# Vision-transformer layer on one core: VectorE's half of the query/key projection becomes a step of its own, one slot behind the products and ScalarE's conversion

## The chip, the core and the metric

One core of a Trainium2 chip runs the whole program. The metric is the device time of one execution in microseconds, as the median of three runs. TensorE (PE in the profile) multiplies, ScalarE (ACT), VectorE (DVE) and GpSimd (POOL) work elementwise, and SyncE (SP) and ScalarE issue the transfers. TensorE writes its results to eight PSUM banks. Each engine works through its own list of instructions in order. Semaphores tie the lists together.

## What is computed

64 images of 12 channels and 224x224 pixels are pooled in patches of 16x16, which gives 196 tokens for each image. A first attention follows, then an expert layer whose second stage contains an attention of 12 heads with 16 dimensions each. What matters here is that second attention:

```python
h = jnp.einsum('becd,fd->becf', xg, w1) + b1          # routed tokens times w1
h = jnp.einsum('becn,becf->bnf', dispatch, h)
x_mlp, x_qkv = (h[..., :MLP_HID], h[..., MLP_HID:])
q, k, v = ...                                         # from x_qkv, 12 heads of 16
attn = jax.nn.softmax(jnp.einsum('bhqd,bhkd->bhqk', q, k) * scale, axis=-1)
x_attn = jnp.einsum('bhqk,bhkd->bhqd', attn, v)
x_mlp = jax.nn.gelu(x_mlp, approximate=False)
```

q and k are kept as two float16 numbers each: the rounded value (high part), and what was rounded away (low part), so that float16 products of three stacked blocks come near float32.

## The kernel before

**Groups, images, slots.** The 64 images go through in 8 groups of 8. The text counts both from 0, so group 2 is the third. The body of a group has 96 slots, 12 for each image, one for each head. In slot h of image i, TensorE makes the products `peak` of head h for image i+1 (line L937). VectorE takes their row maxima (`peaks`, L1459), with which the softmax will be shifted. TensorE also makes the products `score` of head h for image i (L956), and ScalarE takes the exponential (L1155). 8 further slots, the opening of the next group, hold the MLP products `hidden` (L909) with ScalarE's Gelu (L1133), and the peaks of that group's first image.

**The projection.** `project` of image i+2 stands in slot 1 of image i. TensorE computes q and k into two banks (L919). ScalarE rounds each to float16 (L1142, the high part). VectorE subtracts the high part from the bank and writes the low part (L1448), and only then gives the bank back. SyncE waits for both parts, writes them to the scratch tensor `qk_scratch` in HBM (L683), waits for that transfer, and reads six blocks back into the stacks `qs` and `ks` (L689), which the peaks of image i+2 need from slot 0 of image i+1 on. In the opening, `project` of image 1 stands first. For image 0 it stands in the last slots of the group before.

**Banks.** Two of the eight banks serve the peaks in turn (h even, h odd), two the scores. The other four, called the ring, serve everything else. `plan_ring` walks through the list of steps and gives each the ring bank that has been closed longest. TensorE waits before a ring step until the bank's previous user has been read out.

**Fill.** Between peaks and scores stand the other steps: `norm_turn` (L980 on TensorE, then L1470 and L1472 on VectorE, two halves in slots 2 and 3), `norm_back`, `fc2` (L1002), `mix` (L971), and for the next group the pooling of its images: `pool` on VectorE (L1267, seven steps for each tile `xt`, after the last of which the next tile is fetched), and the routing steps (`take`, `norm1`, `first_max` with L1308, `gate_scale` with L1359 and others). Two tables `VECTOR` and `TENSOR` hold a cost for each step in each engine's time. The function `evenly` places the pool steps where the sum of TensorE's costs in a slot exceeds that of VectorE's.

**Peaks and their banks.** The matmul of head h waits until the maxima of head h-2 have been taken, since both use the same bank. VectorE's list in slots 1 to 3 therefore decides when TensorE can start heads 3, 4 and 5.

Of the kernel before, what the change touches and what calls it, by code (L numbers as in the profile page):

```python
# [201 lines left out]
def turning(dg, at):  # L202


    ops = [(at, ("turn_u", dg, 0)), (at + 0.5, ("turn_u", dg, 1)), (at + 1, ("project", dg, 0))]
    return ops + [(at + 1 + 0.5 * i, ("turn_u", dg, i)) for i in range(2, GRP)]


# [25 lines left out]
def opening(dg, tail):  # L234


    plan = []
    last = GRP - 1
    for i in range(GRP):
        ops = []  # L240
        plan.append(ops)
        if tail:
            if i == 0:
                ops.append(("mix", dg - 1, last, H // QUAD - 1))
            if i == 1:
                ops += [("norm_turn", dg - 1, last, half) for half in range(2)]
            if i == 2:
                ops.append(("norm_back", dg - 1, last))
            if 2 <= i < 2 + FC2 // 2:
                ops += [("fc2", dg - 1, last, k) for k in range(2 * (i - 2), 2 * (i - 2) + 2)]  # L250
        if i == 5:
            ops.append(("gate8", dg))
        if i == 0:
            ops.append(("project", dg, 1))
        ops.append(("hidden", dg, i))
        if i == 1:
            ops.append(("values", dg, 0))
        if 1 <= i < 7:
            ops += [("peak", dg, 0, h) for h in range(2 * (i - 1), 2 * (i - 1) + 2)]
        if i == 4:  # L260
            ops.append(("shift", dg, 0, 0))
    ops.append(("shift", dg, 0, 1))
    return plan
# [3 lines left out]
TAKE = 27  # L267
VECTOR = {"peak": 0.52, "choose": 0.95, "first_max": 0.52, "take": 0.9, "norm1_scale": 0.9, "norm1": 0.8, "shift1": 1,
          "stream": 0.9, "stream_norm": 1.2, "gate_scale": 0.2, "gate_logits": 1.8, "gates": 2, "gate_rows": 0.4,
          "chosen": 0.3, "spread": 2.9, "project": 1.3, "norm_turn": 0.65, "fc2": 0.75, "gate8": 1.2, "tok": 0.25}  # L270
TENSOR = {"peak": 0.35, "score": 0.35, "mix": 0.65, "fc2": 0.89, "hidden": 2, "project": 1.33, "values": 0.66,
          "residual": 0.66, "norm_turn": 0.4, "norm_back": 0.34, "shift": 0.2, "turn_u": 0.18, "planes": 1, "tok": 0.15,
          "first_max": 0.66, "first_exp": 0.66, "first_mix": 0.7, "stream": 0.25, "stream_turn": 0.2,
# [3 lines left out]
def body(pool_next, with_next):  # L277
# [3 lines left out]
    for i in range(GRP):  # L281
        fill = [[] for h in range(H)]
# [12 lines left out]
            fill[10] = [("values", 0, i + 1)] + fill[10]  # L295
        if i + 2 < GRP:
            fill[1] = [("project", 0, i + 2)] + fill[1]
        for h in range(H):
            ops = []
            plan.append(ops)  # L300
            if i + 1 < GRP:
                ops.append(("peak", 0, i + 1, h))
            ops.append(("score", 0, i, h))
            ops += fill[h]
            if h in (MIX_LAG, QUAD + MIX_LAG):
                ops.append(("mix", 0, i, h // QUAD - 1))
            if i and h == MIX_LAG - 4:
                ops.append(("mix", 0, i - 1, H // QUAD - 1))
# [7 lines left out]
    front, at = routing(1, TAKE)  # L316
    for slot, op in in_slots(front):
        plan[slot].append(op)
    at = rounds(plan, 1, int(at))
# [4 lines left out]
    at = evenly(plan, pieces * (GRP // PAIR - AHEAD), 0, TAKE - 4)  # L324
# [3 lines left out]
    if pool_next:  # L328
        at = evenly(plan, pieces * AHEAD, TAKE + 1, len(plan) - 3, quiet)
# [8 lines left out]
def ring_of(op):  # L338
    name, key = op[0], op[1:]
    if name == "hidden":  # L340
        ks = [("hid", key + (b,)) for b in range(NF // 2)]
        return ks, ks
    if name == "project":
        ks = [("q", key), ("k", key)]
        return ks, ks
    if name == "mix":
        ks = [("O", key)]
        return ks, ks
    if name == "fc2":
        g, i, k = key  # L350
# [45 lines left out]
def bass_vit_tower(nc, x, cw, Wq, bq, Wk, bk, Wv, bv, w_router, gamma, beta, w1, b1, w2, b2, consts, out):  # L396
# [8 lines left out]
    with ctx:  # L405
# [775 lines left out]
        def _(dve):  # L1181
# [13 lines left out]
            k = 2  # L1195
# [243 lines left out]
                chain(at, dve.tensor_tensor(gate8[:, :, 0:1], cg[:, :, 0:1], gate8[:, :, 1:2], ALU.add))  # L1439
                linked("gate8", 5)  # L1440

            def project(at, G_, dg, i):

                for m in range(2):
                    slot, k_ = at.uses(("qk"[m], (dg, i)))
# [32 lines left out]
            def fc2(at, G_, dg, i, k_):  # L1478
                if k_ == FC2 - 1:
# [3 lines left out]
                    for h in range(2):  # L1483
# [9 lines left out]
                      "first_max": first_max, "shift1": shift1, "stream": stream, "stream_norm": stream_norm,  # L1493
                      "gate_scale": gate_scale, "gate_logits": gate_logits, "gates": gates,
                      "gate_rows": gate_rows, "choose": choose, "chosen": chosen, "spread": spread,
                      "gate8": gates8, "project": project, "peak": peak, "norm_turn": norm_turn, "fc2": fc2})


        @block.gpsimd
# [79 lines left out]
```

How the kernel before makes its waits and increments, by code:

```python
        @block.sync  # L648
# [13 lines left out]
            sp.dma_start(wr_in[:, :], w_router).then_inc(w_in, 16)  # L662
            for m, b in enumerate((gamma, beta)):
                for c in range(2):
                    sp.dma_start(gb[:, m, c:c + 1], b[DC * c:DC * c + DC].rearrange("(p a) -> p a", a=1)) \
                        .then_inc(w_in, 16)
            sp.dma_start(w1_in[:, 0:10, :], w1[0:1280, :].rearrange("(f p) d -> p f d", p=128)).then_inc(w_in, 16)
            sp.dma_start(w1_in[0:F1 - 1280, 10, :], w1[1280:F1, :]).then_inc(w_in, 16)
            sp.dma_start(w2_in[:, :, :], w2.rearrange("(o p) f -> p o f", p=DC)).then_inc(w_in, 16)
            sp.dma_start(b1_in, b1.rearrange("(a f) -> a f", a=1)).then_inc(w_in, 16)
            sp.dma_start(b2_in[:, 0:2, :], b2.rearrange("(a o f) -> a o f", a=1, o=2)).then_inc(w_in, 16)
            sp.wait_ge(su_act, 2)
            sp.dma_start(G[C:2 * C, :], Vp).then_inc(su_dma, 16)
            sp.wait_ge(turn_free, NT - 1)
            sp.wait_ge(su_dve, 4)
# [2 lines left out]
            def project(at, G_, dg, i):  # L678
                n_ = G_ * GRP + i
                sp.wait_ge(hi_ready, 2 * n_ + 2)
                sp.wait_ge(lo_ready, 2 * n_ + 2)
                sp.dma_start(qk_dram[i % 2].rearrange("m s c d (h t) -> (d h) (m s c) t", t=T),
                             qk16[:, :, :, :, :].rearrange("p m s c t -> p (m s c) t")).then_inc(qk_out, 16)
                sp.wait_ge(qk_out, 16 * n_ + 16 + ONE)
                s = i % NSTACK
```

## Time and profile before

| | before |
|---|---|
| median of 3 runs | 1855.82 us (1848.53 to 1863.67) |
| the profiled execution's own time | 1857.67 us |
| its span, first to last instruction | 1855.8 us |
| mean granted TensorE clock | 0.897 |
| TensorE busy | 1525.9 us (82%) |
| VectorE busy | 1215.5 us (65%) |
| ScalarE busy | 846.7 us (46%) |
| GpSimd busy | 249.2 us (13%) |

The profile comes from one execution. Busy means that an instruction of the program was in work. A row of the timeline joins neighbouring instructions of one line; the number in square brackets is the idle time of the engine just before it, and behind the arrow stands what ended it. Shares are means over stages that differ, so that a term of the sum is always read in its own stage.

### The profile page before, as it was taken

Reading aid. Unit: us, or ns where it says so; the run is one execution under the profiler, and the core shown is the slowest. Engines: PE = TensorE matmul, PEld = TensorE weight load, DVE = VectorE, ACT = ScalarE, POOL = GpSimd, SP = SyncE. Lnnn points to the kernel's source line nnn. Section 1 sums busy time; section 2 is a strip of 40 time slices with the busy share of each in tenths; the row PEclk is TensorE's granted clock in tenths of the full one; section 3 lists DMA queues with packets and bytes.
Section 4 is the critical chain, followed back from the end, with each engine's and each line's share of the span. In section 5 each row is a group of like instructions: output and inputs, shape, how many; then the busy total and the mean of one; then the engine's idle time right before and its main releaser. Section 6 shows DMA issues by size and latency. Waiting matters only on the chain.

```text
span 1855.8 us, 34563 instructions
## 1 busy us (share of the span) xinstructions
PE 1525.9 (82%) x12440; PEld 1252.8 (68%) x12440; DVE 1215.5 (65%) x2822; ACT 846.7 (46%) x1935; POOL 249.2 (13%) x318
## 2 busy tenths in 40 slices
PE   4214188998889898998899898989989899989998
PEld 3103176777777677777777677867777687868786
DVE  3366847785877657784877667784777757573552
ACT  1001054544545455544645455544545456545653
POOL 2002101220012001210012001120022101110000
PEclk8556578999999899998999899997899899999999
DMA  3797635542656155542646155642656152101220
GB/s 77 198 231 186 182 82 143 142 131 64 173 128 175 49 150 145 145 128 71 174 128 166 49 154 141 155 121 57 162 137 173 49 150 50 41 25 43 54 57 15
DMA packets 99598, 218.03 MB, mean 117 GB/s; under 512 B 61371, under 2 KB 75877, under 8 KB 88678
## 3 DMA queue, kind: packets, MB, share of 16 engines
q10 hardware_dynamic: 12288, 154.15, 31.5%
q1 hardware_dynamic: 87142, 61.68, 14.4%
q8 instruction: 102, 1.67, 0.4%
q14 instruction: 66, 0.54, 0.1%
HBM read 186.57 MB, written 28.90 MB: 116 GB/s over the span
## 4 chain that ended last, share of the span: by engine, by line
PE 37%; DVE 26%; issue 21%; DMA 7%; POOL 4%; ACT 3%; SPq 0%; DVEq 0%; ACTq 0%; POOLq 0%
DVE psums L1267 9%; DVE peaks L1459 6%; PE bank L1002 6%; PE bank L909 5%; PE bank L971 4%; DMA xt<-in_x_dram 4%; PE bank L919 3%; POOL var L1522 3%; PE bank L937 3%; DMA qs<-shiftT 3%; PE bank L956 2%; PE bank L835 2%; PE bank L819 2%; DVE rows L1403 2%; DVE top L1398 1%
## 5 line engine op out<-in xcount | busy, mean ns | idle before, releaser
L1459 DVE TENSOR_REDUCE peaks<-bank 98x2 f32<-98x392 f32 x768 | 424.6, 562 | 185.8 <-PE bank L937 164.9
L1155 ACT ACTIVATE Pb<-bank 98x392 f32<-98x392 f32 x768 | 374.7, 497 | 290.7 <-PE bank L956 250.1
L1267 DVE TENSOR_REDUCE psums<-xt 112x2 f32<-112x512 f32 x672 | 430.1, 678 | 74.7 <-DMA xt<-in_x_dram 52.6
L937 PE MATMUL bank<-ks,qs 96*98 96x196 f16 x1536 | 265.4, 259 | 59.5 <-DMA ks<-qk_scratch 31.6
L1002 PE MATMUL bank<-w2T,hid 128*98 128x192 f32 x1536 | 301.9, 335 | 0.0
L956 PE MATMUL bank<-qs,ks 97*98 97x196 f16 x1536 | 267.0, 258 | 9.9 <-DMA qs<-shiftT 9.2
L937 PEld LDWEIGHTS bank<-ks,qs 96*98 96x98 f16 x1536 | 165.8, 127 | 143.0 <-DVE peaks L1459 50.4
L1002 PEld LDWEIGHTS bank<-w2T,hid 128*98 128x98 f32 x1536 | 240.3, 170 | 1.7
L971 PE MATMUL bank<-Pb,vals 98*32 98x196 f32 x3072 | 181.5, 357 | 11.6 <-ACT Pb L1155 11.6
L956 PEld LDWEIGHTS bank<-qs,ks 97*98 97x98 f16 x1536 | 167.5, 130 | 20.1 <-DMA qs<-shiftT 10.7
L1448 DVE TENSOR_TENSOR qk<-bank,qk 96x392 f16<-96x392 f32 x128 | 71.8, 561 | 137.9 <-ACT qk L1142 129.5
L1550 POOL TENSOR_TENSOR fin<-fin,both 98x384 f32<-98x384 f32 x64 | 63.8, 997 | 651.9 <-DVE fin L1484 651.9
L909 PE MATMUL bank<-UT,M 104*128 104x196 f32 x768 | 143.6, 338 | 0.0
L909 PEld LDWEIGHTS bank<-UT,M 104*128 104x128 f32 x768 | 132.6, 197 | 2.6 <-issue 2.2
L971 PEld LDWEIGHTS bank<-Pb,vals 98*32 98x32 f32 x3072 | 84.5, 114 | 72.5 <-issue 48.1
L1133 ACT ACTIVATE hid<-bank 128x392 f32<-128x392 f32 x192 | 93.9, 497 | 83.0 <-PE bank L909 82.5
L1513 POOL TENSOR_TENSOR spread_p<-psums,cst 112x196 f32<-112x196 f32 x96 | 49.9, 520 | 595.7 <-DVE psums L1267 595.3
L786 PE MATMUL bank<-spread_p,cst 112*24 112x196 f32 x192 | 49.2, 406 | 97.9 <-POOL spread_p L1513 97.9
L1067 ACT COPY oT<-bank 128x196 f32<-128x196 f32 x192 | 61.9, 322 | 132.0 <-PE bank L971 127.1
L1002 PE MATMUL bank<-w2T,onT 96*98 96x192 f32 (+1 forms) x512 | 106.7, 331 | 8.5 <-ACT onT L1067 8.5
L919 PE MATMUL bank<-UT,M 104*96 104x196 f32 x512 | 111.8, 368 | 0.1
L786 PEld LDWEIGHTS bank<-spread_p,cst 112*24 112x24 f32 x192 | 20.4, 120 | 118.2 <-issue 112.4
(181 smaller groups left out, 1826.2 us busy)
## 6 DMA issues: line engine op xcount, KB each, us to landing
xt<-in_x_dram ACTq DMA_DIRECT2D x96, 1568.0 KB, 8.9
qk_scratch<-qk SPq DMA_DIRECT2D x64, 294.0 KB, 4.1
qs<-qk_scratch SPq DMA_DIRECT2D x192, 73.5 KB, 2.9
ks<-qk_scratch SPq DMA_DIRECT2D x192, 73.5 KB, 3.0
out_dram<-fin SPq DMA_DIRECT2D x64, 147.0 KB
qs<-shiftT SPq DMA_DIRECT2D x128, 2.3 KB
hid<-in_L_ffn_w_dram SPq DMA_DIRECT2D x1, 1440.0 KB
hid<-in_L_ffn_w_dram SPq DMA_DIRECT2D x1, 960.0 KB
```

The lines of the kernel that those rows point to most:

```text
L786: mm = pe.matmul(ps[0:PAIR * C, 0:T], const("plane", PP)[:, PAIR * C * t:PAIR * C * t + PAIR * C], spread_p[:, t, :, :].rearrange("p a b - ...
L909: mm = pe.matmul(ps[:, T * j:T * j + T], M[:, 128 * f:128 * f + 128], UT[:, i, :], start=True, stop=True)
L919: mm = pe.matmul(ps[0:DC, T * c:T * c + T], M[:, f:f + DC], UT[:, i, :], start=True, stop=True)
L937: mm = pe.matmul(peak_ps[s][0:HT, T * q:T * q + T], qs[0:KS, i % NSTACK, h, HT * q:HT * q + HT], ks[0:KS, i % NSTACK, h, :], start=True, s ...
L956: mm = pe.matmul(score_ps[s][0:HT, T * k:T * k + T], ks[:, i % NSTACK, h, HT * k:HT * k + HT], qs[:, i % NSTACK, h, :], start=True, stop=True)
L971: mm = pe.matmul(ps[32 * j:32 * j + 32, 0:T], vals[:, i % 2, q, h, :], Pb[:, (H * i + h) % NP, q, :], start=(q == 0), stop=(q == 1))
L1002: mm = pe.matmul(misc_ps[slot][0:HT, D * h:D * h + D], lhs, w2T[0:w, f, :], start=(f == 0), stop=(f == NF + 1))
L1133: act.activation(hid[:, i, 2 * b:2 * b + 2, :].rearrange("p a b -> p (a b)"), ps[:, 0:2 * T], ACT.Gelu).then_inc(free, 1)
L1155: act.activation(Pb[:, (H * i + h) % NP, :, :].rearrange("p a b -> p (a b)"), score_ps[s][0:HT, 0:2 * T], ACT.Exp, scale=float(DH) ** -0.5 ...
L1267: last = dve.tensor_reduce(psums[:, m % 2, t, 2 * p:2 * p + 2], v[:, 2 * p:2 * p + 2, :, :], AX.XY, ALU.add)
L1448: dve.tensor_tensor(qk16[:, m, 1, :, :].rearrange("p c t -> p (c t)"), misc_ps[slot][0:DC, 0:2 * T], qk16[:, m, 0, :, :].rearrange("p c t ...
L1459: dve.tensor_reduce(peaks[:, h // 6, :, h % 6], peak_ps[s][0:HT, 0:2 * T].rearrange("p (q k) -> p q k", q=2), AX.X, ALU.max, negate=True). ...
```

## The change

`project` stays where it is on TensorE, ScalarE and SyncE. VectorE's function is renamed `low` and becomes a step with a place of its own. For image i+2 that is slot 2 of image i, ahead of `norm_turn`. In the opening it stands behind both halves of `norm_turn`, and in the last slots of a group one slot later than before. The body of VectorE's function is unchanged. The two banks of q and k are opened by `project` and closed by `low`, so that two of the four ring banks are held by them over all steps that lie between. The cost 1.3 moves from the entry `project` of `VECTOR` to an entry `low`, so that `evenly` sees more room in slot 1 and less in slot 2.

```diff
-    ops = [(at, ("turn_u", dg, 0)), (at + 0.5, ("turn_u", dg, 1)), (at + 1, ("project", dg, 0))]
+    ops = [(at, ("turn_u", dg, 0)), (at + 0.5, ("turn_u", dg, 1)), (at + 1, ("project", dg, 0)), (at + 1.8, ("low", dg, 0))]
...
         if i == 0:
             ops.append(("project", dg, 1))
+        if i == 1:
+            ops.append(("low", dg, 1))
         ops.append(("hidden", dg, i))
...
-          "chosen": 0.3, "spread": 2.9, "project": 1.3, "norm_turn": 0.65, "fc2": 0.75, "gate8": 1.2, "tok": 0.25}
+          "chosen": 0.3, "spread": 2.9, "low": 1.3, "norm_turn": 0.65, "fc2": 0.75, "gate8": 1.2, "tok": 0.25}
...
         if i + 2 < GRP:
             fill[1] = [("project", 0, i + 2)] + fill[1]
+            fill[2] = [("low", 0, i + 2)] + fill[2]
...
     if name == "project":
-        ks = [("q", key), ("k", key)]
-        return ks, ks
+        return [("q", key), ("k", key)], []
+    if name == "low":
+        return [], [("q", key), ("k", key)]
...
-            def project(at, G_, dg, i):
+            def low(at, G_, dg, i):
...
-                      "gate8": gates8, "project": project, "peak": peak, "norm_turn": norm_turn, "fc2": fc2})
+                      "gate8": gates8, "low": low, "peak": peak, "norm_turn": norm_turn, "fc2": fc2})
```

**VectorE, slots 0 to 3 of image 0 in a group's body, where image 2 is projected.** `qk16` is the low part, `psums` a pool step, `peaks` the maxima of one head. Before:

```order
L1459 TENSOR_REDUCE peaks<-bank2 98x2
L1459 TENSOR_REDUCE peaks<-bank3 98x2
L1448 TENSOR_TENSOR qk16<-bank4,qk16 96x392
L1448 TENSOR_TENSOR qk16<-bank5,qk16 96x392
L1459 TENSOR_REDUCE peaks<-bank2 98x2
L1267 TENSOR_REDUCE psums<-xt 112x2
L1459 TENSOR_REDUCE peaks<-bank3 98x2
```

After:

```order
L1463 TENSOR_REDUCE peaks<-bank2 98x2
L1463 TENSOR_REDUCE peaks<-bank3 98x2
L1271 TENSOR_REDUCE psums<-xt 112x2 x2
L1463 TENSOR_REDUCE peaks<-bank2 98x2
L1452 TENSOR_TENSOR qk16<-bank4,qk16 96x392
L1452 TENSOR_TENSOR qk16<-bank5,qk16 96x392
L1463 TENSOR_REDUCE peaks<-bank3 98x2
```

The low part now stands behind the maxima of head 2 and ahead of those of head 3. Two pool steps stand where it was; before, one followed head 2.

**TensorE, the first two slots of an opening.** L919 (L923) is the projection of q and k, L909 (L913) one pair of `hidden` products, L980 (L984) one half of `norm_turn`, L926 (L930) the values. Banks 4 to 7 are the ring. Before:

```order
L919 MATMUL bank6<-UT,M 96x196 x2
L919 MATMUL bank4<-UT,M 96x196 x2
L909 MATMUL bank5<-UT,M 128x196 x2
L909 MATMUL bank7<-UT,M 128x196 x2
L909 MATMUL bank6<-UT,M 128x196 x2
L980 MATMUL bank4<-cst,oT 98x128 x3
L980 MATMUL bank5<-cst,oT 98x128 x3
L909 MATMUL bank7<-UT,M 128x196 x2
L909 MATMUL bank6<-UT,M 128x196 x2
L909 MATMUL bank4<-UT,M 128x196 x2
L926 MATMUL bank5<-M,UT 98x192 x2
```

After:

```order
L923 MATMUL bank4<-UT,M 96x196 x2
L923 MATMUL bank7<-UT,M 96x196 x2
L913 MATMUL bank5<-UT,M 128x196 x2
L913 MATMUL bank6<-UT,M 128x196 x2
L913 MATMUL bank5<-UT,M 128x196 x2
L984 MATMUL bank6<-cst,oT 98x128 x3
L984 MATMUL bank5<-cst,oT 98x128 x3
L913 MATMUL bank6<-UT,M 128x196 x2
L913 MATMUL bank5<-UT,M 128x196 x2
L913 MATMUL bank4<-UT,M 128x196 x2
L930 MATMUL bank7<-M,UT 98x192 x2
```

TensorE's steps are the same in the same order, on other banks. Between the projection and the third step of the second image's `hidden`, everything now shares banks 5 and 6.

**VectorE, slots 1 to 3 of image 5, where image 7 is projected.** L1359 (L1363) is `gate_scale`, for whose result GpSimd waits. Before:

```order
L1459 TENSOR_REDUCE peaks<-bank3 98x2
L1448 TENSOR_TENSOR qk16<-bank5,qk16 96x392
L1448 TENSOR_TENSOR qk16<-bank4,qk16 96x392
L1267 TENSOR_REDUCE psums<-xt 112x2
L1459 TENSOR_REDUCE peaks<-bank2 98x2
L1470 RECIPROCAL rden<-bank6 98x12
L1472 TENSOR_TENSOR on_tok<-bank6,rden 98x192
L1359 TENSOR_SCALAR var<-var 98x16
L1459 TENSOR_REDUCE peaks<-bank3 98x2
```

After:

```order
L1463 TENSOR_REDUCE peaks<-bank3 98x2
L1271 TENSOR_REDUCE psums<-xt 112x2 x2
L1463 TENSOR_REDUCE peaks<-bank2 98x2
L1452 TENSOR_TENSOR qk16<-bank7,qk16 96x392
L1452 TENSOR_TENSOR qk16<-bank4,qk16 96x392
L1474 RECIPROCAL rden<-bank6 98x12
L1476 TENSOR_TENSOR on_tok<-bank6,rden 98x192
L1363 TENSOR_SCALAR var<-var 98x16
L1463 TENSOR_REDUCE peaks<-bank3 98x2
```

One more pool step stands ahead of `gate_scale`, and the low part has moved behind head 2.

Elsewhere the pool steps have moved by a slot or two. The one that the prediction speaks of: of the two pool steps in slots 10 and 11 of image 2, one stood on either side of the maxima of image 3's last head, and both stand ahead of it now. An opening holds 15 pool steps in place of 16.

## Rows read from the trace of the kernel before

**Rows 1.** Waits: engine and line, released by, us in total, times, longest.

```profile
PE bank L937 <- DMA ks<-qk_scratch: 31.6, 8, 5.5
...
PE bank L937 <- DVE peaks L1459: 25.0, 35, 2.0
```

**Rows 2.** Groups by line and form: busy us, mean ns, idle before.

```profile
L1267 DVE TENSOR_REDUCE psums<-xt 112x2 f32<-112x512 f32 x672 | 430.1, 678 | 74.7 <-DMA xt<-in_x_dram 52.6 <-DVE peaks L1459 7.6 <-DVE qk L1448 4.8
...
L1448 DVE TENSOR_TENSOR qk<-bank,qk 96x392 f16<-96x392 f32 x128 | 71.8, 561 | 137.9 <-ACT qk L1142 129.5
```

**Rows 3.** Timeline (start, us, engine, line), group 2, projection of image 2.

```profile
688.36 1.27 DVE L1448 TENSOR_TENSOR qk<-bank,qk 96x392 f16<-96x392 f32 x2 [1.33 <-ACT qk L1142]
...
689.77 0.57 DVE L1459 TENSOR_REDUCE peaks<-bank 98x2 f32<-98x392 f32 x1
690.26 0.68 DVE L1267 TENSOR_REDUCE psums<-xt 112x2 f32<-112x512 f32 x1
...
690.39 0.37 PE L937 MATMUL bank<-ks,qs 96*98 96x196 f16 x2 [1.80 <-DVE peaks L1459]
...
691.46 0.37 PE L937 MATMUL bank<-ks,qs 96*98 96x196 f16 x2 [0.53 <-DVE peaks L1459]
```

**Rows 4.** Windows of the same place: busy us by engine, then granted clock.

```profile
688.40:691.80 3.40, 1.08 (x11) 0.68 (x9) 3.11 (x6) 1.59 (x4) 0.00 (x0) 1.00 0.55 132
691.80:695.20 3.40, 3.40 (x26) 1.98 (x24) 1.92 (x4) 1.57 (x4) 0.00 (x0) 0.50 0.25 60
```

**Rows 5.** Timeline of the opening behind group 1.

```profile
656.37 0.56 DVE L1448 TENSOR_TENSOR qk<-bank,qk 96x392 f16<-96x392 f32 x1 [5.26 <-ACT qk L1142]
...
656.86 2.56 PE L909 MATMUL bank<-UT,M 104*128 104x196 f32 x12
...
658.90 1.27 ACT L1133 ACTIVATE hid<-bank 128x392 f32<-128x392 f32 x3
659.25 0.82 PE L980 MATMUL bank<-cst,oT 128*98 128x128 f32 x6
...
659.93 2.23 PE L909 MATMUL bank<-UT,M 104*128 104x196 f32 x12
```

**Rows 6.** Timeline of group 2, projection of image 4.

```profile
730.33 0.56 DVE L1448 TENSOR_TENSOR qk<-bank,qk 96x392 f16<-96x392 f32 x1 [0.39 <-ACT qk L1142]
...
731.39 0.57 DVE L1459 TENSOR_REDUCE peaks<-bank 98x2 f32<-98x392 f32 x1
...
732.66 0.57 DVE L1459 TENSOR_REDUCE peaks<-bank 98x2 f32<-98x392 f32 x1
...
733.67 0.33 PE L937 MATMUL bank<-ks,qs 96*98 96x196 f16 x2
```

**Rows 7.** Timeline of group 2, slot 0 of image 3.

```profile
748.39 0.33 PE L946 MATMUL bank<-cst,peaks 98*6 98x98 f32 x2 [0.53 <-DVEq L1464]
```

**Rows 8.** Timeline of group 2, slots 2 and 6 of image 5.

```profile
804.75 0.18 DVE L1359 TENSOR_SCALAR var<-var 98x16 f32<-98x16 f32 x1
...
805.01 2.90 POOL L1522 TENSOR_TENSOR var<-var,cst 98x16 f32<-98x16 f32 x1 [7.96 <-DVE var L1359]
...
809.83 0.89 PE L1002 MATMUL bank<-w2T,onT 96*98 96x192 f32 x4 [1.25 <-ACT onT L1067]
```

**Rows 9.** Timeline of group 7, the last, projection of image 4.

```profile
1748.46 0.57 DVE L1459 TENSOR_REDUCE peaks<-bank 98x2 f32<-98x392 f32 x1
...
1749.48 0.33 PE L937 MATMUL bank<-ks,qs 96*98 96x196 f16 x2
```

**Rows 10.** Timeline of group 2: image 3's parts out, the six reads, their wait.

```profile
704.42 0.31 SPq L683 DMA_DIRECT2D qk_scratch<-qk  x1
...
711.86 0.31 SPq L689 DMA_DIRECT2D qs<-qk_scratch  x1
...
723.33 0.56 PE L937 MATMUL bank<-ks,qs 96*98 96x196 f16 x2 [5.14 <-DMA ks<-qk_scratch]
```

**Rows 11.** Page, DMA issues: KB each, median us from issue to landing.

```profile
qk_scratch<-qk SPq DMA_DIRECT2D x64, 294.0 KB, 4.1
```

## Prediction, made before the changed kernel had run

> **What bounds the kernel now.** I read the groups by line first. VectorE stands idle 129.5 us in front of the low part L1448, waiting for ScalarE's conversion [rows 2]. That looks like a prize of 7% of the span, but only TensorE's idle time counts, because TensorE is busy 82% of the span. So I read its waits next: what it loses to late maxima is 25.0 us of matmul idle time in all, in 35 places, and 31.6 us in 8 places go to the transfer of the stacks [rows 1]. The question is which of VectorE's 129.5 us are TensorE's too.
>
> The timeline answers it image by image. For image 2 they are: VectorE waits 1.33 us, subtracts until 689.63, takes head 2's maxima at 689.77, and TensorE stands 1.80 us before head 4 and 0.53 us before head 5 [rows 3]. The windows show the consequence: TensorE works 1.08 us of the 3.40 us from 688.4, at the full clock, and the next 3.40 us are granted 0.50, which is 1.2 GHz [rows 4]. Eight groups at 2.33 us make 18.6 us, so most of the 25.0 us is here. The 5.26 us at the opening [rows 5] delay nobody: TensorE runs from 656.86 to 662.16 without an idle microsecond between its rows. For the other images VectorE waits 0 to 1.6 us at the low part, as at image 4 [rows 6], and no wait of TensorE for the maxima of head 4 by more than about 0.2 us follows: there the wait is filled time that costs nothing.
>
> **The change, part by part.** The same 128 subtractions of 0.56 us run [rows 2]. No transfer is added. What changes is who stands behind whom.
>
> *Image 2 (gain).* Without the low part, VectorE is free at 687.03, that is 688.36 less the 1.33 idle. Two pool steps of 0.68 [rows 2] now fill the wait, to 688.4; head 2's maxima take 0.57, to 688.95, and TensorE starts head 4 at 689.0 rather than 690.39. Then comes the low part, 1.27 us to 690.2, then head 3's maxima to 690.8, and TensorE starts head 5 at 690.85 rather than 691.46 [rows 3]. The wait moves from head 4 to head 5, and 0.6 us a group is left of the 2.33. The low part ends 0.6 us later, so its stack does too. In four groups that stack landed with less than 1 us to spare and in two it was already waited for, which takes back a part. I take -4 us for 8 groups, between 0 and -5. The clock is a further question, a rival below: TensorE would still stand still for some 1.6 of 2.3 us, which I take as too little better to keep the clock up.
>
> *The opening (loss).* q and k hold two ring banks until both halves of `norm_turn` are through VectorE. The first image's third `hidden` product now shares bank 5 with its first, and must wait for the first Gelu, which ends at 658.90 + 0.50 = 659.4. Before, it had q's bank, free at 656.93, and its four matmuls began near 658.6 in the run of twelve that ends at 659.42 [rows 5]: +0.9 us. Those four then end near 660.35, and their Gelu takes 0.5, to 660.9. The second half of `norm_turn` uses the same bank, and TensorE would be ready for it at 660.5: +0.4. The second image's `hidden` needs both banks of `norm_turn` read by VectorE, another 0.2 to 0.3. The sum is 1.65 us, with bounds 0.9 (only the Gelu wait stays) and 1.9. Behind it TensorE is busy nearly without a break, so nothing gives it back. Seven openings at 1.65 and the first at 1.0 (no `norm_turn`) make +12.6 us. A rule of the Trainium skill speaks against the change here as well: its page "Perfetto Trace Analysis", section "Matmul Optimizations", asks that all eight PSUM banks be used so that work can overlap. By it, the loss is every step that finds fewer free banks; by the rows, only the opening has consecutive ring steps so dense that it is felt, and the sum is as above.
>
> *Image 4 (loss).* Before, the low part ended at 730.89, in time that VectorE had free since the projection came late; then head 2's maxima at 731.39, head 3's at 732.66, done 733.23, ahead of TensorE's head 5 at 733.67 [rows 6]. Now the low part, 1.27 us, and the 0.14 us behind it (689.63 to 689.77 in [rows 3]) stand between head 2 and head 3, whose maxima end at 733.23 + 1.41 = 734.64. TensorE's head 5 waits 1.0 us. The tiny steps of routing behind it go 1.4 us later and could add 0.4 (they feed a GpSimd step that TensorE waits for). Bounds 0 and 1.4, since a later wait for another cause could swallow it; I take 1.0 in seven groups, +7 us.
>
> *Slot 0 of image 3 (loss).* TensorE already waits 0.53 us there for the maxima of the last head of the image before [rows 7]. One more pool step, 0.68, now stands ahead of them; about 0.6 shows. Pool steps of this stretch exist in six groups: +3.5 us, bounds 0 and 4.
>
> *Image 7 (loss).* `gate_scale` at 804.75 starts GpSimd's 2.90 us, on which `gate_logits`, then ScalarE's exponential, then the copy onT hang, for which TensorE waits 1.25 us at 809.83 [rows 8]. One pool step more stands ahead, and the low part has only changed places: +0.7 us in six groups, +4 us, bounds 0 and 4.5.
>
> *The last group (loss).* No pool steps fill anything. Image 4's head 3 ends its maxima at 1749.03, head 5 starts at 1749.48 [rows 9]. The low part's 1.41 us go in between, less 0.4 that I allow for head 2 coming earlier, since it no longer waits for the low part: head 3 ends at 1750.05. That is +0.57 us for images 3 to 7, +3 us, bounds 0 and 4.
>
> *Images 3, 5 and 6 (nothing).* VectorE waited 0.1 to 0.8 us there; the pool step gained and the low part lost cancel within 0.3 us. SyncE issues image 3's write at 704.42, and the reads at 711.86, 7.4 us later [rows 10]; the write shares the engines with a tile fetched on ScalarE's queue, and lands with it. Issued 1 to 1.6 us later it still has 5.8 us, more than the median write's 4.1 [rows 11], so the stall of 5.14 us stays as it is. The cover is that fetch; without it, the full 1 to 1.6 us would show in six groups, +6 to 10 us.
>
> Sum: -4 + 12.6 + 7 + 3.5 + 4 + 3 = +26 us. The profiled execution took 1857.67 (span 1855.8 and 1.9 around it), 1.85 above the median, so 1855.8 + 26 = 1882 us. Low bounds: -5 + 7 + 0 = 1858. High bounds: 0 + 14.5 + 10 + 4 + 4.5 + 4 = +37, 1893.
>
> **The rivals.** *Swallowed.* Each loss lands just ahead of a wait for something else and vanishes, and only the opening's Gelu wait, 8 x 0.9 = 7 us, and the gain of 4 stay: 1859. For it: TensorE idles a sixth of the span in all. Against it: between the places named its rows follow each other closely. *The clock pays (faster).* At image 2 TensorE does four `peak` matmuls sooner, the 3.40 us at clock 0.50 do not follow, and up to half of them, 1.7 us, comes back, in up to seven groups: -12 us, with the gain of 5 -17. It decides the sign once the losses stay under 17 us, as when the opening costs 0.9 and image 4 nothing: 1855.8 - 17 + 7 = 1846; with no loss at the banks at all, 1839. Against it: at that place the stack of image 2 has less than 1 us to spare in four groups, so that TensorE would run into that transfer. The Trainium skill ("TensorE: Matmul & The Clock Gate", section "What's actually happening") says that the clock falls back after idleness and not by chance; the trace agrees, 1.08 us of work in 3.40 ahead of the fall. *The stack grows late.* The write of image 3 is pushed behind the fetch: 1882 + 8 = 1890, and more where image 2's stack joins it, to 1900. *Nothing moves on VectorE.* ScalarE's part is so late that the low part still waits where it stands now: only the bank costs are left, 1868. Against it: at image 2 ScalarE releases VectorE at 688.36 [rows 3], before VectorE would come to it at 688.95.
>
> **How the numbers follow.** Chances: the forecast 0.54 (1866 to 1893), swallowed 0.2 (1850 to 1866, with the variant in which nothing moves on VectorE), the clock pays 0.16 (1828 to 1850), the stack grows late 0.1 (1893 to 1905). Predicted is the first, 1882. The range 1846 to 1897 leaves out most of the third and half of the fourth, 2 in 10. A measurement of this kernel tells about 1%, 18.6 us, from no change: faster is below 1837.3, slower above 1874.4. Slower: 0.42 of the forecast and 0.1, 0.52. Faster: 0.1, from the third. Same: 0.38.
>
> **What would show it.** In the changed profile the low part's idle time should fall from 137.9 us to under 70. TensorE's wait for the maxima should leave head 4 of image 1's row and appear at head 5 there (about 1.2 us) and at image 4 (1.0). In each opening a wait of the L909 matmuls for ScalarE's Gelu of 0.7 to 0.9 us should be new. The wait of L946 at slot 0 of image 3 should be about 1.1, that for onT about 1.9. The prediction is wrong if the openings keep their length, or if the 0.50 stretch behind image 2 is gone in most groups.

## The result, and the profile after

| | before | after |
|---|---|---|
| median | 1858.82 us (4 runs, 1848.53 to 1863.67) | 1882.88 us (4 runs, 1870.31 to 1887.49) |
| ratio | | 1.0137, 95% interval 1.0096 to 1.0179 |
| the profiled execution, its span | 1857.67, 1855.8 us | 1884.72, 1882.9 us |
| mean granted clock in it | 0.897 | 0.901 |
| VectorE's low part: busy, idle before it | 71.8, 137.9 us | 71.4, 61.2 us |

The changed kernel is slower by 24 us. Some executions of either kernel are in a slower state, and every comparison below leaves them out. VectorE waits 77 us less in front of the low part (61.2, forecast under 70), and TensorE, busy 82% of the span in both, gets none of it.

Groups by line and form of the changed kernel (busy us, mean ns, idle before), answering [rows 2]:

```profile
L1452 DVE TENSOR_TENSOR qk<-bank,qk 96x392 f16<-96x392 f32 x128 | 71.4, 558 | 61.2 <-ACT qk L1146 51.2
```

TensorE's waits in the changed kernel (us in total, times, longest), answering [rows 1]:

```profile
PE bank L790 <- POOL spread_p L1517: 95.6, 12, 26.7
PE bank L941 <- DMA ks<-qk_scratch: 37.7, 13, 5.6
...
PE bank L941 <- DVE peaks L1463: 22.4, 50, 1.0
...
PE bank L913 <- ACT hid L1137: 6.6, 6, 1.9
...
PE bank L1006 <- DVEq L1457: 3.6, 12, 0.4
...
PE bank L984 <- ACT hid L1137: 1.8, 7, 0.3
```

The maxima are waited for oftener and shorter (longest 1.0 for 2.0 us). The transfer of the stacks is waited for in 13 places instead of 8, and three rows of bank and Gelu waits are new. For spread_p the sum is lower only because the part ahead of the loop differs from run to run; its count went from 6 to 12.

Timeline of group 2, projection of image 2 (start, us, engine, line), answering [rows 3]:

```profile
696.68 1.26 DVE L1452 TENSOR_TENSOR qk<-bank,qk 96x392 f16<-96x392 f32 x2
...
696.82 0.37 PE L941 MATMUL bank<-ks,qs 96*98 96x196 f16 x2 [0.21 <-DVE peaks L1463]
...
698.71 0.37 PE L941 MATMUL bank<-ks,qs 96*98 96x196 f16 x2 [1.04 <-DVE peaks L1463]
...
707.38 0.37 PE L941 MATMUL bank<-ks,qs 96*98 96x196 f16 x2 [1.67 <-DMA ks<-qk_scratch]
```

Windows of the same place (busy us by engine, granted clock, DMA share, GB/s), answering [rows 4]:

```profile
696.60:700.00 3.40, 2.04 (x17) 1.36 (x20) 2.95 (x7) 2.09 (x6) 0.00 (x0) 1.00 0.33 74
700.00:703.40 3.40, 3.40 (x50) 2.15 (x42) 3.40 (x7) 2.97 (x8) 0.00 (x0) 1.00 0.21 47
```

The wait of 1.80 us at head 4 is gone (0.21), that at head 5 has grown from 0.53 to 1.04, and image 2's stack is now waited for, 1.67 us in this group. In the first window TensorE works 2.04 us, for 1.08 before, and its clock does not fall to 1.2 GHz behind it here.

The opening behind group 1, answering [rows 5]:

```profile
663.26 1.49 PE L913 MATMUL bank<-UT,M 104*128 104x196 f32 x8
...
665.25 0.89 ACT L1137 ACTIVATE hid<-bank 128x392 f32<-128x392 f32 x2
665.80 0.93 PE L913 MATMUL bank<-UT,M 104*128 104x196 f32 x4 [1.05 <-ACT hid L1137]
...
666.57 0.49 PE L984 MATMUL bank<-cst,oT 128*98 128x128 f32 x3
667.32 0.53 PE L984 MATMUL bank<-cst,oT 128*98 128x128 f32 x3 [0.26 <-ACT hid L1137]
667.93 2.34 PE L913 MATMUL bank<-UT,M 104*128 104x196 f32 x12
...
668.66 1.27 DVE L1452 TENSOR_TENSOR qk<-bank,qk 96x392 f16<-96x392 f32 x2
...
670.78 0.50 PE L941 MATMUL bank<-ks,qs 96*98 96x196 f16 x4
```

From the first `hidden` product to the first peaks of the new group's first image (L941) the opening takes 7.52 us, for 5.78 before, where these peaks start at 662.64. Up to `norm_turn` it is 3.31 us (663.26 to 666.57) for 2.39, and from there to the second image's `hidden` 1.36 for 0.68 (659.25 to 659.93 in [rows 5]):

```profile
662.64 0.50 PE L937 MATMUL bank<-ks,qs 96*98 96x196 f16 x4
```

**Where the time went, image by image.** The table lists, summed over the groups, by how much each stretch from one image's first `peak` matmul to the next image's is longer than in the first profile of before. Each number comes from the starts of these matmuls in the timelines and is good to about 0.5 us. Stretch 7 holds the first part of the next opening too, up to the new group's first peaks; what follows, up to image 1's, is equal in all kernels. (The expectations call a stretch an image's period: that of image 6 is stretch 6.)

```
stretch                   1      2      3      4      5      6      7
before, second profile  -0.8   -2.0   -0.3    0.0   +1.4   +0.3   -4.1
changed                 -8.7   -2.4   +7.7   +5.4   +1.5  +14.8  +14.0
changed, second         -5.4   -6.1  +10.1   +5.5   +1.7  +13.1   +7.9
e1_open_back            +5.1   -0.5   +6.8   +5.4   +1.3  +13.1   +1.8
e2_open_only            +2.0   -2.3    0.0    0.0   -0.4   +0.4  +13.6
e3_cost_back            -2.0   +1.5  +10.6   +0.7   +2.1   +2.8   +4.3
e4_cost_only           +20.9   -1.4   -2.3   +4.9   -2.0  +13.9   -8.3
f1_planes_later         -7.7   -5.1   +9.2   +5.4   +1.4   +5.2   +9.4
f2_image2_only          -2.1   -2.5   +3.2   +0.1   +0.6   -1.2   +1.9
f3_banks_only           +2.1   +0.6   +1.2   +0.1    0.0   +0.5   +8.9
f4_image4_back          +3.5   +0.2   -1.9   +2.0  +10.7   +5.9   +5.4
g1_image2_pool          -4.4   +0.4   +0.1    0.0   +0.3   +0.2    0.0
```

Stretches 3 to 6 repeat within about 2.5 us between two profiles of one kernel. Stretches 1, 2 and 7 hold most of the falls of the clock and repeat only within about 6 us. The part ahead of image 0's first peaks took 240 to 253 us, and is not in the table, nor is the first opening, which lies in it.

### The profile page after: what moved, and what is told of

It is laid out like the page before. It is cut to its first block, busy times and chain, and to the rows that moved or that the text cites. A ratio compares the mean times of both kernels' runs of the same rounds, so it can differ in the third digit from the quotient of the medians.

```text
span 1882.9 us, 34563 instructions
## 1 busy us (share of the span) xinstructions
PE 1537.9 (82%) x12440; PEld 1250.0 (66%) x12440; DVE 1216.1 (65%) x2822; ACT 849.5 (45%) x1935; POOL 248.7 (13%) x318
## 3 DMA queue, kind: packets, MB, share of 16 engines
q10 hardware_dynamic: 12288, 154.15, 30.4%
q8 instruction: 102, 1.67, 0.4%
## 4 chain that ended last, share of the span: by engine, by line
PE 42%; DVE 23%; DMA 14%; issue 13%; POOL 3%; ACT 2%; SPq 2%; DVEq 0%; POOLq 0%; ACTq 0%
PE bank L1006 7%; DVE psums L1271 6%; DVE peaks L1463 6%; PE bank L913 5%; PE bank L975 5%; PE bank L923 4%; DMA ks<-qk_scratch 4%; DMA xt<-in_x_dram 3%; PE bank L941 3%; DMA qk_scratch<-qk 3%; PE bank L960 3%; DMA qs<-shiftT 3%; PE bank L839 2%; POOL var L1526 2%; PE bank L790 2%
## 5 line engine op out<-in xcount | busy, mean ns | idle before, releaser
L941 PE MATMUL bank<-ks,qs 96*98 96x196 f16 x1536 | 265.2, 259 | 62.1 <-DMA ks<-qk_scratch 37.7
L1006 PE MATMUL bank<-w2T,hid 128*98 128x192 f32 x1536 | 305.4, 338 | 3.7 <-DVEq L1457 3.6
L941 PEld LDWEIGHTS bank<-ks,qs 96*98 96x98 f16 x1536 | 164.3, 126 | 148.7 <-issue 49.4
L1006 PEld LDWEIGHTS bank<-w2T,hid 128*98 128x98 f32 x1536 | 242.0, 171 | 8.7 <-DVEq L1457 6.7
L913 PE MATMUL bank<-UT,M 104*128 104x196 f32 x768 | 147.5, 342 | 7.6 <-ACT hid L1137 6.6
L913 PEld LDWEIGHTS bank<-UT,M 104*128 104x128 f32 x768 | 132.1, 197 | 15.2 <-ACT hid L1137 9.0
L790 PE MATMUL bank<-spread_p,cst 112*24 112x196 f32 x192 | 49.1, 405 | 95.6 <-POOL spread_p L1517 95.6
L1006 PE MATMUL bank<-w2T,onT 96*98 96x192 f32 (+1 forms) x512 | 106.4, 330 | 8.8 <-ACT onT L1071 8.8
L923 PE MATMUL bank<-UT,M 104*96 104x196 f32 x512 | 112.8, 370 | 0.1
L1452 DVE TENSOR_TENSOR qk<-bank,qk 96x392 f16<-96x392 f32 x128 | 71.4, 558 | 61.2 <-ACT qk L1146 51.2
L790 PEld LDWEIGHTS bank<-spread_p,cst 112*24 112x24 f32 x192 | 20.4, 120 | 116.2 <-issue 110.4
```

Source lines behind the costliest of these rows:

```text
L790: mm = pe.matmul(ps[0:PAIR * C, 0:T], const("plane", PP)[:, PAIR * C * t:PAIR * C * t + PAIR * C], spread_p[:, t, :, :].rearrange("p a b - ...
L913: mm = pe.matmul(ps[:, T * j:T * j + T], M[:, 128 * f:128 * f + 128], UT[:, i, :], start=True, stop=True)
L923: mm = pe.matmul(ps[0:DC, T * c:T * c + T], M[:, f:f + DC], UT[:, i, :], start=True, stop=True)
L941: mm = pe.matmul(peak_ps[s][0:HT, T * q:T * q + T], qs[0:KS, i % NSTACK, h, HT * q:HT * q + HT], ks[0:KS, i % NSTACK, h, :], start=True, s ...
L1006: mm = pe.matmul(misc_ps[slot][0:HT, D * h:D * h + D], lhs, w2T[0:w, f, :], start=(f == 0), stop=(f == NF + 1))
L1452: dve.tensor_tensor(qk16[:, m, 1, :, :].rearrange("p c t -> p (c t)"), misc_ps[slot][0:DC, 0:2 * T], qk16[:, m, 0, :, :].rearrange("p c t ...
```

## The experiments

Each edit is shown against the changed kernel. The kernel before ran beside every one.

**e1_open_back.** Only the body keeps the change. One pool step of the opening moves back behind `norm_turn` with the low part.

```diff
-..., (at + 1.8, ("low", dg, 0))]
+..., (at + 1, ("low", dg, 0))]
-            ops.append(("project", dg, 1))
-        if i == 1:
-            ops.append(("low", dg, 1))
+            ops += [("project", dg, 1), ("low", dg, 1)]
```

> The changed kernel with only the openings put back: there the low part follows its projection at once, as before; the body and the pool steps stay as in the changed kernel. Theory A (the forecast's sum): the openings cost 12.6 us, so this kernel gives them back and stands at about 1870 us, ratio 1.007 to before. Theory B (the two traces side by side): the new waits that can be seen in the openings are 1.05 + 0.26 us in seven of them, 9 us; the rest of the loss lies in the body, about 15 us of it at image 6's period, which is 2.2 us longer in most groups; so the ratio is 1.009. If the openings cost nothing, it stays at 1.0137.

Measured 1.0123 (1.0065 to 1.0181). The waits of the openings are gone and stretch 7 is 6 to 12 us shorter than in the two profiles of the changed kernel, as both theories had it. The time hardly shows it: in this profile stretch 1 is 10 to 14 us longer, with nearly the same waits but five falls of the clock near image 2, for two. Stretch 1 has 58 us at 1.2 GHz, for 13 and 22 in the changed kernel's profiles. The six runs of e1 agree with that: their mean granted clock is 0.893, for 0.901. The interval holds both theories and also 1.0137, an opening that costs nothing; the time alone decides nothing.

**e2_open_only.** Only the openings keep it. They are not quite the changed kernel's: one pool step more stands ahead of `norm_turn`, and the plan hands out other banks.

```diff
-            fill[1] = [("project", 0, i + 2)] + fill[1]
-            fill[2] = [("low", 0, i + 2)] + fill[2]
+            fill[1] = [("project", 0, i + 2), ("low", 0, i + 2)] + fill[1]
```

> The kernel before with only the openings changed: there the low part stands behind norm_turn, in the body it follows its projection at once; pool steps as before. Theory A: +12.6 us, ratio 1.0068. Theory B: +9 us, ratio 1.005. A rival, that an opening's loss is given back further on, gives 1.000 to 1.002. In the profile the L913 matmuls should wait about 1.05 us for ScalarE's Gelu in each opening by A and B both.

Measured 1.0092 (1.0057 to 1.0126): the openings cost 17 us, between 11 and 23, and theory A's 12.6 is inside, B's 9 is not. All other stretches stay within 2.3 us, so that nothing gives it back. The wait for the Gelu was expected as 1.05 us in each opening; it stands in five of the seven between groups, from 0.52 to 1.05. The timeline behind group 1:

```profile
658.39 0.93 PE L912 MATMUL bank<-UT,M 104*128 104x196 f32 x4 [0.52 <-ACT hid L1136]
...
659.91 0.54 PE L983 MATMUL bank<-cst,oT 128*98 128x128 f32 x3 [0.26 <-ACT hid L1136]
...
662.64 0.93 PE L912 MATMUL bank<-UT,M 104*128 104x196 f32 x4 [0.48 <-DVEq L1456]
```

Three waits stand there, 1.26 us together. The first two are those of the prediction's sum. The last is not: the prediction's third is a wait for `norm_turn`'s banks, and here the second image's third pair of `hidden` products waits for the low part to give back its second bank. It is there in all seven openings, 0.5 us each, and B's sum had left it out. In the plan of this kernel that pair gets k's bank, given back last; in the changed kernel's loop it gets q's, given back 0.6 us sooner, and waits nothing.

**f3_banks_only.** The banks are handed out as in the changed kernel, but VectorE does the low part at once, and the table is as before. The step `low` stays in the plan and only closes the banks there.

```diff
-"low": 1.3, "norm_turn"
+"project": 1.3, "norm_turn"
-"gate8": gates8, "low": low,
+"gate8": gates8, "project": low,
```

> The changed kernel's distribution of the ring banks with VectorE's work as before: the low part is done right behind the projection, but the banks of q and k are handed out as if it were done where the change has it. Pool steps as before. Theory A (banks): hidden's third product still shares its bank with the first and waits 1.05 us for the Gelu in each opening, so that the openings lose the 9 to 12.6 us, and nothing else is lost, ratio 1.005 to 1.007. Rival D (the late subtraction itself delays the openings, through the maxima or the stack): 1.000.

Measured 1.0054 (1.0023 to 1.0084), as theory A has it. Nothing is late on VectorE, and the waits for the Gelu are there all the same, while stretches 1 to 6 stay as before:

```profile
PE bank L913 <- ACT hid L1137: 5.4, 6, 1.1
...
PE bank L984 <- ACT hid L1137: 1.7, 7, 0.3
```

So most of the openings' loss, 10 us (between 4 and 16) of e2's 17, is the price of two banks held open in the plan. The profiles say the same more closely. From the first `hidden` product to the new group's first peaks, the seven openings between groups take 42.1 and 42.4 us in all in the two profiles of before, 52.5 in f3's, 53.7 and 53.8 in the changed kernel's, and 57.9 in e2's (some begin at 1.2 GHz, so that 52.5 and 53.7 hardly differ). What e2 has beyond f3 comes only with the late subtraction: 0.5 us of it in each opening is the wait above.

**e3_cost_back and e4_cost_only.** The low part late but the pool steps where they were, and the reverse. `room` is a step that does nothing and only carries the cost.

```diff
-"low": 1.3, "norm_turn"
+"project": 1.3, "norm_turn"
```

> The changed kernel with the cost table as before: the low part is where the change puts it on VectorE, the pool steps and what hangs on them (the planes of a pair of images, the next fetches) are back in the slots that they had before. Theory A: the pool steps cost 3.5 us at slot 0 of image 3 and 4 us at image 7, so this kernel stands 7.5 us below the changed one, ratio 1.0097. Theory B: the planes that stand one slot early (67 for 68) and wait 0.88 us for GpSimd's spread_p, and the 0.5 us for the maxima behind them, are the pool's doing; with the table back 1.5 us a group go, 12 us, ratio 1.007. If the order of the low part alone makes the loss, it stays at 1.0137.

```diff
-            fill[1] = [("project", 0, i + 2)] + fill[1]
-            fill[2] = [("low", 0, i + 2)] + fill[2]
+            fill[1] = [("project", 0, i + 2), ("low", 0, i + 2)] + fill[1]
+            fill[2] = [("room", 0, i + 2)] + fill[2]
...
-"low": 1.3, "norm_turn"
+"room": 1.3, "norm_turn"
```

with the openings' low part put back and a `room` in its place.

> The kernel before with only the pool steps moved: the low part follows its projection at once everywhere, but the table counts its 1.3 us one slot later, so that the pool steps stand where the changed kernel has them. Theory A: the two pool steps in slots 1 of an image now stand with the low part and delay the maxima, about as the changed kernel's 7.5 us, ratio 1.004. Theory B: +12 us and more, ratio 1.0065, with the wait of L790 for spread_p of about 0.9 us in slot 7 of image 5. If the planner's moves are harmless by themselves, 1.000.

Measured 1.0157 (1.0093 to 1.0221) and 1.0131 (1.0066 to 1.0195). Each costs about as much as the whole change, so the two parts don't add up. Both results lie above what either theory gave, though A's 1.0097 for e3 is just inside the interval. So is 1.0137, the case in which the order of the low part makes the whole loss. The stretches speak against that case. Stretches 4 and 6 lengthen with the pool steps' move (+4.9 and +13.9 in e4) and hardly without it (+0.7 and +2.8 in e3). Stretch 3 lengthens with the low part (+10.6) and not with the pool steps (-2.3). At image 2 the two belong together: in e4 two pool steps stand behind a low part that still waits for ScalarE, and head 4 waits 3.25 us in place of the 1.80 of [rows 3]. That makes 20.9 us in stretch 1, most of e4's whole loss and nothing that the changed kernel has: the waits for maxima at heads 4 and 5 grow by 6 us only, but the clock falls in all eight groups and stays at 1.2 GHz for 84 us, for 40 and 41 before. For e3, the profiled execution is its fastest of six (1868.31 us, median 1878.47); its stretches add up to 20 us, where the ratio gives 29.

```profile
697.71 0.56 PE L941 MATMUL bank<-ks,qs 96*98 96x196 f16 x2 [3.25 <-DVE peaks L1463]
```

**f1_planes_later.** In the changed kernel the step `planes` (L790) stands in slot 7 of image 5, one slot early, and waits for GpSimd's spread_p:

```profile
818.80 0.89 PE L1006 MATMUL bank<-w2T,onT 96*98 96x192 f32 x4 [1.26 <-ACT onT L1071]
...
822.07 1.16 PE L790 MATMUL bank<-spread_p,cst 112*24 112x196 f32 x6 [0.88 <-POOL spread_p L1517]
...
829.18 0.34 PE L941 MATMUL bank<-ks,qs 96*98 96x196 f16 x2 [0.50 <-DVE peaks L1463]
```

```diff
-    ops += [(slot + 2.2, ("planes", dg, m)), (slot + 3.4, ("tok", dg, m))]
+    late = 1 if int(slot) == 65 else 0
+    ops += [(slot + 2.2 + late, ("planes", dg, m)), (slot + 3.4 + late, ("tok", dg, m))]
```

> The changed kernel with one step put back by one slot: the planes of the third pair of images (and the tokens made of them) stand in slot 68, as before the change, while the pool steps stay where the changed kernel has them. Theory B (the planner's move of the planes makes image 6's period 2.2 us longer): the 0.88 us wait for spread_p and the 0.5 us for the maxima behind it go, the period falls back to about 20.6 us from 22.5, and the whole to 1.0137 less 11 us, ratio about 1.008. Rival C: the pool step in slot 66 delays spread_p itself and the wait only moves by one slot: the period stays above 22 us.

In the profile theory B holds. L791 (the L790 above) starts in the next slot without a wait, and stretch 6 is 21.2 us in the middle groups, for 22.5, which makes 8 to 10 us in all (20.6 had been expected; the rest stays):

```profile
806.33 1.14 PE L1007 MATMUL bank<-w2T,hid 128*98 128x192 f32 x6
807.40 1.18 PE L791 MATMUL bank<-spread_p,cst 112*24 112x196 f32 x6
```

The ratio, 1.0129 (1.009 to 1.0169), is above the 1.008 expected: four runs don't tell these 8 us from the run-to-run spread, and the gain is shown in the stretch only.

**f4_image4_back.** e3, and image 4's low part at once. The table's line is that of e3.

```diff
-            fill[1] = [("project", 0, i + 2)] + fill[1]
-            fill[2] = [("low", 0, i + 2)] + fill[2]
+            if i != 2:
+                fill[1] = [("project", 0, i + 2)] + fill[1]
+                fill[2] = [("low", 0, i + 2)] + fill[2]
+            else:
+                fill[1] = [("project", 0, 4), ("low", 0, 4)] + fill[1]
```

> The changed kernel with the cost table as before (no pool step moves), and in addition the low part of image 4 put back behind its projection. Theory A: image 4's late low part costs 7 us (1.0 in seven groups), so that this kernel stands 7 us below the same one without that, whose ratio was 1.0157 (1.0093 to 1.0221); in the profile the period from image 3's first peak to image 4's falls by 1.0 to 1.3 us a group and the 0.38 us wait of L1006 for the bank goes. Rival: something else in that period takes its place, the stall in front of image 3's or image 5's stack above all, and the sum stays.

Measured 1.0113 (1.0071 to 1.0156), not distinct from e3. Stretch 3 is 12.5 us shorter: the waits that the low part had brought there (0.38, 0.37 and 0.21 us, below) are all gone. But stretch 5 grows by 8.6: the banks fall differently behind image 4, and a step of routing (L842) waits for one that a late low part still holds (its release is L1460), 0.74 us in each of six groups and 0.54 in a seventh, 5.0 us; two falls of the clock (7 us at 1.2 GHz, for none) make most of the rest.

```profile
789.25 0.91 PE L842 MATMUL bank<-tm,aT 128*98 128x196 f32 x4 [0.74 <-DVEq L1460]
```

The rival holds with another cause than the stack that it named.

**f2_image2_only and g1_image2_pool.** The low part late for image 2 alone, first with the pool steps as before, then (g1) with its cost counted in slot 2. In g1 two pool steps stand in slot 1 of image 0 and none in slot 2, for none and one. Three more move as well, against what was expected: in image 1, slots 0 and 5 hold one less each and slot 1 one more. No `planes` moves. Both kernels put the openings back as e1 does, and f2 the table as e3 does.

```diff
-            fill[1] = [("project", 0, i + 2)] + fill[1]
-            fill[2] = [("low", 0, i + 2)] + fill[2]
+            if i == 0:
+                fill[1] = [("project", 0, 2)] + fill[1]
+                fill[2] = [("low", 0, 2)] + fill[2]
+            else:
+                fill[1] = [("project", 0, i + 2), ("low", 0, i + 2)] + fill[1]
```

> The kernel before with the low part one slot later for image 2 alone, where VectorE was seen to wait 1.33 us and TensorE 2.33 us with it; everything else and every pool step as before. By the forecast's sum this part alone gains 4 us (0 to 5), ratio 0.998. The rival that the clock pays gives up to 12 us more where the fall behind image 2 is avoided, ratio 0.991. If the later stack takes all of it back, 1.000. In the profile the wait of L941 for the maxima at head 4 of image 1 should go from 2.0 us to 0.3, that at head 5 rise to about 1.0, and the wait for ks be new at slot 0 of image 2.

Measured 0.9998 (0.997 to 1.0025). The waits at heads 4 and 5 go from 2.0 and 0.5 to 0.15 and 1.6 us (0.3 and 1.0 had been expected), and the sum of stretches 1 and 2 falls by 4.6 us against the first profile of before, 1.8 against the second. The stack is waited for in three groups. The forecast's 4 us is inside the interval, and so is nothing.

> The kernel before with the low part one slot later for image 2 alone, and its cost counted there, so that the three pool steps around it move too (two in slot 1, none in slot 2, as in the changed kernel) and all others stay, the planes too. The theory that adds up the waits: at image 2 the wait at head 5 is 1.0 us where it is 1.6 us with the pool steps unmoved, so that one more 0.6 us a group is gained, unless the stack takes it (its wait at slot 0 of image 2 grows to about 1.1 us); with the 4 us of the low part 4 to 9 us in all, ratio 0.995 to 0.998. If the clock no longer falls there, as in six of eight groups of the changed kernel's profile, 8 us more, 0.991. If the stack takes all, 0.998 to 1.000.

Measured 0.995 (0.992 to 0.998), median 1844.74 us: g1 beats both kernels. Group 2, head 5 and the stack:

```profile
679.58 0.45 PE L942 MATMUL bank<-ks,qs 96*98 96x196 f16 x2 [1.26 <-DVE peaks L1464]
...
688.59 0.37 PE L942 MATMUL bank<-ks,qs 96*98 96x196 f16 x2 [0.55 <-DMA ks<-qk_scratch]
```

Over eight groups the waits for the maxima in stretch 1 fall from 19.1 to 9.7 us, and the stack takes 2.4 of it and the maxima of image 2's head 4 another 4.1, behind the pool step that moved to slot 1 of image 1. That leaves 3 us of the 9 that the runs gained. From the first image on, g1's profile is as long as the second profile of before, within 1 us. The rest would fit the clock, 0.898 in the mean of g1's runs for 0.892 beside them, and no profile shows where. The clock still falls at image 2 in six groups.

**g2_after_again and g3_before_again.** Both kernels unchanged, for second profiles.

> The changed kernel once more, for a second profile. If the low part's place decides the clock at image 2, this profile too shows the fall to 1.2 GHz behind it in at most two of eight groups and a sum of the images' 1 periods near 9 us under before's. If it is a matter of the run, four to seven groups show it, as with the first experiment's kernel, whose body is the same, and the sum is up to 14 us higher. The periods of images 3 to 6 should repeat within 0.3 us a group.

> The kernel before once more, for a second profile: what differs from the first is what one profile can't tell. If the fall behind image 2 belongs to the kernel, seven of eight groups show it again; if not, fewer. The part ahead of the first image should differ by some us (252.4 in the first profile, 240 to 253 in the others), the periods of images 3 to 6 by less than 0.3 us a group.

Measured 1.0118 (1.0073 to 1.0162) and 0.9998 (0.9962 to 1.0033). The fall of the clock near image 2 comes in seven of eight groups in both profiles of before, and in two in both of the changed kernel, so that it belongs to the kernel. It does not belong to the low part's place alone: e1, with the same body, has five, and g1, with the same order on VectorE around image 2, six. f1, which differs from the changed kernel only at image 5, has three. Every kernel that has the openings, the low part at image 2 or the pool steps around it as before has five or more (f2 five; e2, e3, f3 and f4 six; e4 eight). So the falls are missing only where all three are changed together. This rests on one profile of most kernels.

## Why the prediction was right

The forecast was 1882 us and slower by over 1%, and 1882.88 was measured. That the number fits this closely is luck. Below, "measured" is the mean of the changed kernel's two profiles less that of before's two. One term was 10 us short, the clock's gain of about 10 us (an estimate, below) was not counted, and the two nearly cancel. Of the forecast's two signs of being wrong, one came true: the stretch at 1.2 GHz behind image 2 is gone in most groups, from seven of eight to two. The direction and most of the losses were right for the reasons given; the clock at image 2 was not.

- **Image 2.** Forecast -4; stretches 1 and 2 together give -9.9. At the maxima the mechanism was as forecast: head 4's wait of 2.0 becomes 0.27, head 5's 0.5 becomes 1.0, 9.5 us less in all. The low part's later stack was mis-sized: it is waited for in seven groups, 8.8 us for 1.1, where "less than 1 us to spare" in four groups had only promised a part. By these waits alone the gain is 2 us. What makes it larger is the clock: stretch 1 has 13 and 22 us at 1.2 GHz in the changed kernel's two profiles, for 40 and 41. The step that failed is the forecast's "too little better to keep the clock up".
- **The opening.** Forecast 12.6. Stretch 7 gives +13.0, and by itself (e2) the change costs 17, between 11 and 23. f3 shows the cause to be the banks for most of it. In the seven openings between groups, the time to the new group's first peaks grows by 11.5 us in all, about 1.75 in most of them, where 1.65 had been forecast. By the starts behind group 1, the first image's `hidden` takes 0.92 us more (forecast 0.9) and `norm_turn` up to the second image's `hidden` 0.68 more (0.6 to 0.7). The rows of waits show 1.05 and 0.26 of it. So this term held part by part, in that opening; the fit has some luck in it, as before's begins there at 1.2 GHz and the changed one's does not, which hides about 0.4 us (an estimate from matmuls 0.33 us apart at the start, for 0.17). In the last opening TensorE also waits 0.49 us for the low part's second bank. The first opening was mis-sized: it waits 1.90 us for the Gelu (1.0) and takes 8.6 us, for 5.3, which the stretches don't hold. "Only the opening" has ring steps dense enough for the banks to be felt, the prediction said. The row of L1006 above shows 12 waits for the low part's bank in the body, 3.6 us.
- **Image 4.** Forecast 7, and 0.6 in the last group. Stretch 3 gives +9.0, and f4, against e3, takes it all back. The size was right and the place mostly wrong: head 5 waits 0.21 us, not 1.0, because TensorE is already late by 0.38 us for the bank that the low part still holds, and 0.64 us, for 0.27 before, goes to routing further on.

```profile
739.46 1.22 PE L1006 MATMUL bank<-w2T,hid 128*98 128x192 f32 x6 [0.38 <-DVEq L1457]
740.89 0.37 PE L941 MATMUL bank<-ks,qs 96*98 96x196 f16 x2 [0.21 <-DVE peaks L1463]
```

- **Slot 0 of image 3.** Forecast 3.5 and a wait of about 1.1 us in the place of the 0.53 of [rows 7]. It is 1.12, in six groups; stretch 4 gives +5.4, and e3 shows that it goes with the pool steps.

```profile
756.16 0.33 PE L950 MATMUL bank<-cst,peaks 98*6 98x98 f32 x2 [1.12 <-DVEq L1468]
```

- **Image 7.** Forecast 4, measured +13.8 in stretch 6. This term was 10 us short. The wait for onT is still 1.26 us, not 1.9, yet the pool step's 0.6 us is lost: counted from the image's first peaks, the L1006 matmuls start 12.16 us on (806.64 to 818.80), for 11.56 before, since the 0.16 us bank wait and 0.29 us at head 5 delay TensorE as much as the chain. What the forecast lacked is the step behind it: `planes` follows its last pool step by a fixed 2.2 slots. The pool step moved to an earlier slot and ran 0.6 us later all the same, and TensorE came for its result a slot too soon: 0.88 us, and 0.5 at the next image's first peaks. The prediction counted the pool steps that moved and never asked what hangs on them.
- **The last group.** Forecast 3, in stretches 3 to 7; in stretches 3 to 6 its own share is 2.1 us (0.7, 0.6, 0.2, 0.6), and head 5 waits 0.44 us.
- **Images 3, 5, 6.** Forecast 0. Image 3 is projected in stretch 2, where a wait of 0.44 us for the maxima at head 5 is new in all eight groups, 3.5 us; stretch 5 gives +0.9, and the stall at image 3's stack is 29.0 us in six groups, for 30.4.
- **The clock.** Counted as a rival of 12 us. It did pay at image 2, beside the losses and not in their place. The changed kernel's eleven runs had a mean granted clock of 0.901, the 24 of before that ran beside the last experiments 0.892. Among these 24 the time falls by 12 us for each 0.01 of clock, which by that slope makes 10 us (an estimate). So about 34 us were lost and 10 came back, where the forecast had 26 and nothing. The profiles don't show these 10 us. From the first peaks of the first image to those of the last, before has 188 and 174 us at 1.2 GHz, the changed kernel 184 and 188: what is gained in stretch 1 comes back in stretch 7 (126 and 123 us, for 106 and 92). In them the stretches add up to +32.

Of the rivals, "swallowed" is excluded by e2 alone. "Nothing moves on VectorE" is excluded by the low part's idle time, 61.2 us for 137.9, and by head 4's wait. "The stack grows late" occurred at image 2, and the forecast's zero for image 3's stack held. e1 hardly gains although stretch 7 shortens, because the clock at image 2 falls again; why it does so, in a kernel with the same body, is open.

## What to carry to other kernels

A step split in two holds its banks over everything in between, and the openings paid for that with a wait for ScalarE, which the split had not touched. When a planner's cost moves, follow not only the steps it places but those placed relative to them, and look at where each producer then ends in time. Delay a step only at the one place where its engine's idle time is also the bottleneck's: at one image of eight here the runs gained 0.5%, of which the waits explain a third, while the change everywhere cost 1.4%.

## What the runs showed of the hardware

Most of the spread between executions of one kernel goes with the clock. 24 runs of before lie between 1836.67 us at a mean granted clock of 0.905 and 1863.32 at 0.883, and the correlation of time and clock is -0.90. Two other sets of before, 16 and 21 runs, give -0.92 and -0.86, and 14 and 10 us for each 0.01, for 12 here. A difference of 0.01 in the clock therefore goes with as much time as most terms of this sum have, and one profile doesn't tell it.

The part ahead of the first image took 240 to 253 us in thirteen profiles, and 252 and 245 in the two of the unchanged kernel. That spread is half of the effect studied, so that spans of two profiles should be compared from the first image on.
